# Masked attention scores from a bf16 accumulation on TensorE, with the old and new maximum from one scan

## The reference, cut to what matters

```
h = x @ W[r];  s = h @ a_src[r];  d = h @ a_dst[r]
e = leaky_relu(s[src] + d[dst], 0.2)     # masked to edges of relation r
m = segment_max(e, dst)                  # per (node, relation)
w = exp(e - m[dst]);  denom = segment_sum(w, dst)
out += segment_sum((w / denom[dst])[:, None] * h[src], dst) + b[r]
```

## Time and profile before

| | |
|---|---|
| median of 3 runs (range) | 3840.04 us (3839.91 to 3840.69) |
| span of the profiled execution | 3833.0 us |
| `attention` in the span | about 136 to 1740 us |
| busy in the span | PE 74%, DVE 60%, POOL 60%, ACT 38% |
| granted TensorE clock, mean | 0.756 of full speed over the span, 0.59 in `attention` |

### The profile page before, as it was taken

How to read it: one execution, slowest core, us unless ns; L and a number is a source line. 1 busy time by engine, 2 the same in 40 slices (tenths; PEclk the granted TensorE clock), 3 DMA queues, 4 the chain that set the end, 5 groups by cost and what they waited for, 6 DMA issues and landing times. The chain is left out here.

```text
span 3833.0 us, 77662 instructions
## 1 busy us (share of the span) xinstructions
PE 2849.0 (74%) x16134; PEld 1989.3 (52%) x16135; DVE 2312.7 (60%) x8562; ACT 1473.1 (38%) x3352; POOL 2309.6 (60%) x1835
## 2 busy tenths in 40 slices
PE   7277777777777776565889897878887787877863
PEld 4155555555555554342344365656666565656651
DVE  7299989989999997685242254343444434343433
ACT  1055555555555554341000043433433333333431
POOL 0277666766676666430000048888888888888882
PEclk7565655656555665567989979988888999898986
DMA  4544434444443445884332335555555555555544
GB/s 135 100 112 114 125 106 111 123 109 111 125 112 109 119 115 94 85 162 117 107 105 78 111 40 55 53 55 53 54 54 53 55 53 55 52 54 53 53 46 91
DMA packets 661597, 336.51 MB, mean 88 GB/s; under 512 B 436912, under 2 KB 625123, under 8 KB 660580
## 3 DMA queue, kind: packets, MB, share of 16 engines
q0 software_dynamic: 148736, 86.57, 23.6%
q1 hardware_dynamic: 447430, 110.13, 14.0%
q10 hardware_dynamic: 65248, 138.05, 9.7%
HBM read 156.42 MB, written 202.84 MB: 94 GB/s over the span
## 5 line engine op out<-in xcount | busy, mean ns | idle before, releaser
L2181 POOL DMA_INDIRECT sums<-el_rows,el_idx x816 | 1269.2, 1555 | 611.8 <-DVE el_rows L2395 363.5
L820 POOL DMA_INDIRECT at_hs<-table,at_rec_s x976 | 1032.7, 1058 | 506.9 <-PE near_ps L961 301.6
L858 ACT CAST at_count_s<-near_ps 128x400 f16<-128x400 f32 x976 | 482.5, 494 | 686.7 <-PE near_ps L961 624.3
L961 PE MATMUL near_ps<-at_pair_hot,at_src_low_hot 128*128 128x425 f16 x976 | 486.2, 498 | 349.4 <-ACT at_count_s L858 268.2
L2393 DVE CAST el_idx<-el_place 128x4 uint32<-128x4 f32 x204 | 35.3, 173 | 837.5 <-DMA sums<-el_rows,el_idx 806.2
L933 PEld LDWEIGHTS sums_ps<-at_hw,at_hit 128*128 128x128 f32 x1952 | 461.5, 331 | 20.7 <-issue 14.8
L933 PE MATMUL sums_ps<-at_hw,at_hit 128*128 128x66 f32 x1952 | 441.7, 408 | 8.3 <-DVE acc L1007 8.3
L961 PEld LDWEIGHTS near_ps<-at_pair_hot,at_src_low_hot 128*128 128x128 f16 x976 | 134.5, 138 | 507.3 <-ACT at_count_s L858 348.5
L2329 ACT ACTIVATE el_h<-el_h_ps,el_valid 128x128 f32<-128x128 f32 x816 | 232.6, 368 | 248.1 <-PE el_h_ps L2243 248.1
L999 DVE TENSOR_SCALAR at_pair_hot<-iota_wide,at_rec_s 128x400 f16<-128x400 f16 x976 | 322.0, 332 | 2.4
L2197 PE MATMUL el_miss_t<-ident_b,el_miss 128*128 128x128 bf16 x816 | 84.7, 266 | 290.6 <-DVE el_miss L2367 290.6
(11 more groups left out here) (374 smaller groups left out, 4973.7 us busy)
## 6 DMA issues: line engine op xcount, KB each, us to landing
slots<-at_count_s ACTq DMA_DIRECT2D x122, 850.0 KB
el_rec<-attr SPq DMA_DIRECT2D x816, 32.0 KB
chunk<-slots SPq DMA_DIRECT2D x256, 100.0 KB
attr<-in_edge_attr SPq DMA_DIRECT2D x19, 1248.0 KB
chunk<-slots ACTq DMA_DIRECT2D x208, 100.0 KB
at_rec_s<-meta SPq DMA_DIRECT2D x992, 3.5 KB
at_hs<-table,at_rec_s POOLq DMA_INDIRECT x976
el_pair<-meta SPq DMA_DIRECT2D x816, 1.0 KB
```

Of the source, the lines that this page charges most:

```text
L820: pool.indirect_dma_start(hs[:, s, u, :], None, k.table, bass.IndirectOffsetOnAxis(rec[:, s, u, 0:1].bitcast(U32), 0)).then_inc(gathered[s ...
L858: a.copy(count[:, (n.o + d) % 2, i, 0:AW], near[:, (n.o + d) % 2, 0:AW]).then_inc(count_ready, 1)
L961: pe.matmul(near[:, s, 0:SW], low_hot[:, s, i, :], pair_hot[:, s, i, :], start=False, stop=True, skip_group_check=(i > 0)).then_inc(near_r ...
L2181: pool.indirect_dma_start(k.sums_flat[a], bass.IndirectOffsetOnAxis(idx[:, j, a:a + 1], 0), rows[:, j, a, :], None, compute_op=ALU.add).th ...
```

## The change

The masked scores are no longer made by DVE and turned by PE; PE builds them in turned form. For each visit it accumulates two bf16 matmuls in PSUM: `miss` (now bf16) against a diagonal of -BIG, and a selector of 32 rows, `sel`, against the scores of the batch, which lie in turned form in `score_t` (32 rows: 8 visits by 3 bf16 parts and a zero). `far` and its operation go. The three parts are split once, by POOL in `edge_keys`, and stored with the row (TW = 68). In `attention` DVE copies them out (`flat`), PE turns them with one matmul (`turn_scores`, 32 columns of output), ACT copies the result to SBUF (`scores`). The maximum goes straight into a table `self_top` that interleaves it with the loop's score; one scan of 16 elements over that and an interleaved `fresh` gives old and new maximum of each visit together, and leaky_relu is taken of both in one operation. DVE waits for the gather two batches ahead, where it waited one batch ahead before. `gather_sums` and `acc` have 65 columns instead of 66.

Core of the diff:

```diff
-TW = D + 2
+FW = D + 1
+TW = D + 4
+SB = 4 * B
...
+            step = Steps(pool, split_step)
+            for t in range(NT):
+                pool.wait_ge(row_ready, 3 * t + 3)
+                value, rest = score[:, t, 0, :], score_rest[:, t % 2]
+                split = rows[:, t % 4, :, D + 2:TW].bitcast(BF16)
+                step(nc.gpsimd.tensor_copy(split[:, :, 0], value))
+                step(nc.gpsimd.tensor_sub(rest, value, split[:, :, 0]))
+                step(nc.gpsimd.tensor_copy(split[:, :, 1], rest))
+                nc.gpsimd.tensor_sub(split[:, :, 2], rest, split[:, :, 1]).then_inc(split_ready, 1)
...
-        miss = sb("miss", [P, 2, B, P])
-        far = sb("far", [P, 2, B, P])
+        miss = sb("miss", [P, 3, B, P], BF16)
+        flat = sb("flat", [P, 2, B, 4], BF16)
+        score_t = sb("score_t", [SB, 2, P], BF16)
...
+            def scores(n, d):
+
+                act.wait_ge(score_turned, n(1, d + 1))
+                a.copy(score_t[:, (n.o + d) % 2], score_ps[:, (n.o + d) % 2]).then_inc(score_copied, 1)
...
                 if h == 0:
-                    pe.wait_ge(far_ready, n(1, d + 1))
+                    pe.wait_ge(key_step, n(2, 2 * d + 2))
+                    pe.wait_ge(score_copied, n(1, d + 1))
                     if n.after(1 - d):
                         pe.wait_ge(top_ready, n(1, d))
                 for u in range(4 * h, 4 * h + 4):
-                    t = pe.transpose(masked[:, u, :], far[:, (n.o + d) % 2, u, :], k.ident[:])
-                t.then_inc(masked_ready, 1)
+                    pe.matmul(masked[:, u, :], miss[:, (n.o + d) % 3, u, :], k.big_ident[:], start=True, stop=False)
+                    m = pe.matmul(masked[:, u, :], k.sel[:, u, :], score_t[:, (n.o + d) % 2, :], start=False, stop=True)
+                m.then_inc(masked_ready, 1)
+
+            def turn_scores(n, d):
+
+                pe.wait_ge(flat_ready, n(1, d + 1))
+                pe.matmul(score_ps[:, (n.o + d) % 2, :], flat[:, (n.o + d) % 2].rearrange("p u i -> p (u i)"),
+                          k.ident_b[:], start=True, stop=True).then_inc(score_turned, 1)
...
-                    v.tensor_reduce(top[:, s, 1:B + 1], masked[:], AX, ALU.max).then_inc(top_ready, 1)
-                if n.has(1):
-                    q = (n.o + 1) % RING
-                    dve.wait_ge(gathered[q], (n.round(1) + 1) * (16 * B))
-                    dve.wait_ge(key_step, n(2, 4))
-                    if n.after(1):
-                        dve.wait_ge(hit_ready, n(2))
-                    v.scalar_tensor_tensor(far[:, w], miss[:, w], -BIG, hs[:, q, :, D + 1:D + 2].to_broadcast([P, B, P]),
-                                           ALU.mult, ALU.add).then_inc(far_ready, 1)
+                    v.tensor_reduce(k.self_top[:, vis, 1], masked[:], AX, ALU.max).then_inc(top_ready, 1)
...
-                    v.tensor_tensor(top[:, s, 1:B + 1], top[:, s, 1:B + 1], k.dst_v[:, vis], ALU.add).then_inc(best_step, 1)
+                    v.tensor_tensor_scan(run[:, s].rearrange("p u i -> p (u i)"),
+                                         k.fresh[:, vis, :].rearrange("p u i -> p (u i)"),
+                                         k.self_top[:, vis, :].rearrange("p u i -> p (u i)"), run[:, w, B - 1, 1:2],
+                                         ALU.add, ALU.max).then_inc(best_step, 1)
...
+                    dve.wait_ge(gathered[q], (n.round(2) + 1) * (16 * B))
+                    v.tensor_copy(flat[:, m], hs[:, q, :, D + 2:TW].bitcast(BF16)).then_inc(flat_ready, 1)
```

More of the change, by code:

```diff
@@ L242, in _ @@
                 nc.gpsimd.tensor_add(fold[:], fold[:], k.ident[:, 16 * j:16 * j + 16]).then_inc(fold_const, 1)
+            step = Steps(pool, sel_step)
+            nc.gpsimd.memset(rows[:, :, :, D + 2:TW], 0.0).then_inc(sel_step, 1)
+            nc.gpsimd.memset(k.big_ident[:], 0.0).then_inc(sel_step, 1)
+            step.n += 2
+            step(nc.gpsimd.memset(k.sel[:], 1.0))
+            step(nc.gpsimd.affine_select(out=k.big_ident[:], in_=k.big_ident[:], compare_op=ALU.not_equal, fill=-BIG,
+                                         base=0, pattern=[[-1, P]], channel_multiplier=1))
+            step(nc.gpsimd.affine_select(out=k.sel[:], in_=k.sel[:], compare_op=ALU.is_ge, fill=0.0, base=0,
+                                         pattern=[[-4, B], [0, P]], channel_multiplier=1))
+            step(nc.gpsimd.affine_select(out=k.sel[:], in_=k.sel[:], compare_op=ALU.is_ge, fill=0.0, base=3,
+                                         pattern=[[4, B], [0, P]], channel_multiplier=-1))
+            step = Steps(pool, split_step)
[7 more added lines that the diff above has]
+                nc.gpsimd.tensor_sub(split[:, :, 2], rest, split[:, :, 1]).then_inc(split_ready, 1)
         @block.vector
@@ L846, in hits @@
                 if h == 0:
-                    act.wait_ge(far_ready, n(1, 1))
+                    act.wait_ge(key_step, n(2, 2))
                     if n.after(2):
                         act.wait_ge(sums_ready, n(1, -1))
-                a.activation(hit[:, s, half], far[:, s, half], ACT.Identity, bias=k.ones_f[:, 0:1],
-                             scale=1.0 / BIG).then_inc(hit_ready, 1)
+                a.activation(hit[:, s, half], miss[:, n.o % 3, half], ACT.Identity, bias=k.ones_f[:, 0:1],
+                             scale=-1.0).then_inc(hit_ready, 1)
+            def scores(n, d):
+                act.wait_ge(score_turned, n(1, d + 1))
+                a.copy(score_t[:, (n.o + d) % 2], score_ps[:, (n.o + d) % 2]).then_inc(score_copied, 1)
             def keep(n, d, i):
@@ L868, in step @@
                     keep(n, 1, 0)
+                    scores(n, 1)
                     keep(n, 1, 1)
@@ L932, in gather_sums @@
                 for u in range(4 * h, 4 * h + 4):
-                    m = pe.matmul(sums[:, u // 4, (u % 4) * TW:(u % 4 + 1) * TW], hit[:, s, u, :], hw[:, s, u, :],
+                    m = pe.matmul(sums[:, u // 4, (u % 4) * FW:(u % 4 + 1) * FW], hit[:, s, u, :], hw[:, s, u, :],
                                   start=True, stop=True)
@@ L968, in step @@
                     counts(n, 1, 0)
+                    turn_scores(n, 1)
                 if n.has(-2):
@@ L1007, in update @@
                 v.scalar_tensor_tensor(a, a, fade[:, (n.o + d) % 3, u:u + 1],
-                                       sums[:, u // 4, (u % 4) * TW:(u % 4 + 1) * TW], ALU.mult, ALU.add
+                                       sums[:, u // 4, (u % 4) * FW:(u % 4 + 1) * FW], ALU.mult, ALU.add
                                        ).then_inc(acc_step, 1)
@@ L1014, in step @@
                 vis = bass.ds(n(B), B) if here else None
-                fresh = k.fresh[:, bass.ds(n(1), 1), :].rearrange("p a u -> p (a u)") if here else None
                 if here:
@@ L1044, in step @@
                 if here:
-                    dve.wait_ge(best_step, n(3, 2))
-                    v.tensor_tensor_scan(run[:, s], fresh, top[:, s], run[:, w, B:B + 1], ALU.add, ALU.max).then_inc(best_step, 1)
+                    dve.wait_ge(best_step, n(2, 2))
+                    v.scalar_tensor_tensor(lrelu[:, s], lrelu[:, s], SLOPE, lrelu[:, s], ALU.mult,
+                                           ALU.max).then_inc(parts_step, 1)
                 if back:
```

104 lines of the change are left out of this document (49 added, 55 removed).

## The result

The changed kernel takes **4058.39 us** (median of 4 runs, 4054.54 to 4061.75) against 3839.97 before (4 runs): a ratio of 1.0575, 95% interval 1.056 to 1.059. The forecast was 3991 in a range of 3880 to 4090. Direction and range held, but the forecast was 67 us low, and the result lies outside the 3930 to 4050 that it gave for its own case. Ahead of the prediction these 7 us were put down to what lies around the span. That is about 2 us only, by the four executions of after (4061.75 against a span of 4059.9); the other 5 are that the profiled execution of before was shorter than the median one.

The account below looks back on a forecast made before the run. DVE bounds attention by 0.2 us over PE's 11.25; PE's need becomes 13.5 a batch. 106 batches at +1.3 give +138, with +10 and +3 span 3984, plus 7 to the median: 3991 us, range 3880 to 4090.

Parts of the forecast that it names:

- its own case: The main case: with row switches between 0.10 and 0.16 us the kernel takes 3930 to 4050 us; 55%.
- What bounds the kernel: In attention DVE bounds by 0.2 us and its loop-turn stall; the change cuts DVE's need from 11.46 to 9.9 a batch.
- Changes of rows: In scores each switch between 128 and 32 rows costs PE 0.135 us; 16 a batch make 2.16 us.
- Change of columns: At turn_scores only the columns change, which costs nothing; the matmul itself adds 0.11 us a batch.
- The clock: In attention some 18% at 2.4 GHz could make the halves about 0.25 us cheaper; set against other batches' waiting.
- PE's need of 11.25: In attention before the change, PE with its chain of counts needs 11.25 us a batch by itself.
- the clock rises: Rival: longer unbroken PE stretches in attention raise the clock; PE needs about 12.5 us a batch, whole about 3880; 20%.
- dearer than read: Rival: attention takes 14.2 us a batch if full-clock stretches go, and its end adds 28 us: about 4085; 12%.
- The sum: 106 attention batches at +1.3 us give +138; with +10 and +3 the span is 3984, plus 7 to the median, 3991.
- the tail: Attention from about 1500 us: slower batches first fill stalls of unused visits' gathers; 0 to 28 us, taken as 10.
- The start: POOL's split takes 1.15 us a tile, less than PE's tile; with two tables written at a stride, 3 us in all.
- Changes of rows cost nothing: Rival: row switches in scores are free, PE needs 11.4 us a batch, the whole takes about 3770, faster; 10%.

Follow-up runs that it names:

- pad128: The changed kernel with all operands of scores and turn_scores filled up with zeros to 128 x 128: 3781.6 us, ratio to before 0.9849.
- nosplit: The changed kernel without POOL's split of the scores into three parts at the start (parts stay zero): 4035.8 us.
- hold: The changed kernel with one wait more: DVE begins its two large one-hot operations only when POOL has split the first 12 tiles: 4067.4 us.
- best: The changed kernel with operands padded to 128 x 128 and the three score parts made by DVE in attention, not POOL; table 66 columns: 3787.5 us.

## Why the prediction was right, and where its sizes were off

**What bounds the kernel.** Right. DVE's load fell as forecast: in after it is busy 143.0 us in 200 / 13.94 batches, 9.97 each, in pad128 172.7 in 200 / 11.40, 9.84 each, and I had 9.9. It was worth nothing in after, since PE paid for it: DVE waits 3.4 us at each maximum, for `hit_t`, as the prediction wanted, and from 300 to 1500 us PE has no wait for DVE.

**Changes of rows.** The mechanism is shown by four kernels. Its size was 0.11 us, not the 0.135 that I took from two f32 operands of a later stage. Sixteen cost 1.79 in the batch shown (4.20 - 2.41), where the sum had 2.16.

**Change of columns: a step that failed.** I read from the earlier trace rows that a change from 64 to 128 columns costs nothing, and carried it over to one from 128 to 32 and back. It costs 0.25; with `turn_scores` itself the stretch grew by 0.55 where I had 0.11. Those rows are of another pair of sizes, in f32 and at the full clock, and I should have kept two ends open, nothing and twice the 0.135 of a change of rows.

**The clock.** I set "18% at 2.4 GHz" against "other waiting" and took the difference as zero. That was the second failure. The batch of the earlier trace rows from which I took PE's need of 11.25 has its own fast stretch: from count 5, at 908.64, a count lasts 0.35 instead of 0.56. In after no stretch at 2.4 GHz is left, and the part from count 4 to `carries` takes 4.58 instead of 4.30 (on average over 400 to 1400 us 4.61 instead of 4.42). The rival "the clock rises" had the sign wrong, "dearer than read" named just this loss, though at 14.2 a batch it put too much on it; the 4058 measured lie nearer to its 4085 than to the forecast. The clock did rise, to 0.65, in pad128, once the changes were gone. PE is busier in after (166.5 of 200) than in pad128 (155.9), at a lower clock. Why the changes, or what comes with them, keep the clock down, stays open.

Together, for the batch shown: 11.25 + 1.79 + 0.55 + 0.28 + 0.03 = 13.90 (forecast 13.5), the last term being from `carries` to count 0.

**The sum.** The forecast had +138 up to the tail, +10 in it and +3 at the start. Measured are 200.1 from first to last maximum and 26.4 at the start. The last maximum ahead of the first long stall of the tail is the one 107 batches after the first. In before and in after it starts at

```profile
1498.28 1.21 DVE L1019 TENSOR_REDUCE at_top<-masked 128x8 f32<-128x1024 f32 x1
```

```profile
1718.18 1.22 DVE L1062 TENSOR_REDUCE self_top<-masked 128x1024 f32 x1 [3.43 <-ACT at_hit_t L869]
```

so these 107 grew by (1718.2 - 231.2) - (1498.3 - 204.8) = 193.5, or 1.81 each where the sum had 1.3. The last 14 grew by 7, where 14 x 1.74 would have been 24: that slower batches fill the stalls of the gathers before they add to them was right, and so was its size. So +55, -3 and +23 are the three misses, and 3984 + 75 = 4059 is the span measured. The 7 us that the forecast added from span to median were wrong, as said above: the median of after lies 1.5 below the profiled span. That made the miss of the median, 67, smaller than that of the sum, and was luck. The two sizes that were too small, columns and clock, were partly covered by the one that was too large, rows.

**The start: a resource that was not in the sum.** "Four dependent operations a tile, 4 x 0.29 = 1.15 us, less than what PE takes for a tile" priced POOL by the earlier trace rows, which is a stretch in which DVE waits. I asked what stands behind POOL's chain, but not what runs beside it. The price was 22.6 us, which nosplit and hold show.

**The rivals.** "Changes of rows cost nothing" had 3770 as its time if the switches were free. Where padding really makes them free the time is 3782, with 22.6 us of the start in it: about 3759 without it. So the arithmetic was near and the condition wrong.

## What to carry to other kernels

Before mixing matmuls with short and long contractions, look at the tile that each works with: at 1.2 GHz every change of it cost 0.11 us here, as much as the 128 columns themselves, and filling the short operand up with zeros to 128 x 128 made it free, turning a kernel that was 5.8% slower than the old one into one that is 1.5% faster. Before giving a small operation to POOL, look at what DVE runs in the same microseconds, and if they collide make the ring deep enough that nobody waits, rather than moving the work to the engine that is nearly full. And where a need is read from one batch, check whether that batch ran at the clock that the rest will have.

## What the hardware showed

- A change between 128 and 32 rows in bf16 at 1.2 GHz: 0.11 us in either direction. Between 128 and 32 columns: 0.14 in, 0.11 out. Eight matmuls with weights of their own and pairs that add into one region, all 128 x 128: 0.107 each, nothing more.
- The granted clock in `attention` was 0.50 in each of the kernels with changes of rows in `scores`, and 0.59 to 0.65 in those without. PE was the busier in the former (82 to 84% against 75 to 77%, 300 to 1500 us). No run separates the changes from what comes with them.
- A POOL operation on 128x8 in SBUF took 0.20 us with DVE idle and 13.04 beside a DVE operation with two SBUF inputs, ending within 0.1 us of it.
- The stall of DVE at the loop's turn shrank when three small operations were taken away (81.9 to 62.5 us in 18 times) and a second one came when three were added (40.1 us in 35 times). In the kernel before, each of the 16 stalls between 300 and 1500 us holds a packet of the DMA queue of the kind "instruction", of which there are 98 in these 1200 us; of the 17 second stalls of over 1 us in the same window of best only 3 do. That the first kind of stall is a wait for instructions is a guess from this, and no run tests it.
